# The first head's query remainder: from a VectorE subtraction to a TensorE matmul and a ScalarE copy

## What is computed

```python
x = x + tanh(g_xattn[0]) * xattn(layernorm(x), ctx, ctx, mask, Wq, Wk, Wv, Wo, 16)
x = x + tanh(g_ffn[0]) * ffn(layernorm(x), Wg, bg, W1, b1, W2, b2)
# xattn: 16 heads of 64, softmax(q k^T + mask) v, then Wo
# ffn: softmax over 8 experts, the best 2 of them, relu(x W1 + b1) W2 + b2, weighted
```

## Time and profile before

| | |
|---|---|
| median of 3 runs | 1154.83 us (1151.76 to 1156.01) |
| profiled execution | 1155.27 us, its span 1153.5 us |
| mean granted TensorE clock | 0.921 of full speed |
| busy: TensorE, VectorE, ScalarE, GpSimd | 881.5, 939.9, 785.6, 710.6 us |
| queries' low halves (L726) | 256, 681 ns each, 173.7 us |
| queries' high halves (L545) | 256, 599 ns each, 152.9 us |

### The profile page before, as it was taken

One profiled execution on the slowest core, in us unless ns is written; L12 is line 12 of the kernel. 1 busy time (PEld: TensorE's weight loads), 2 busy tenths in 40 slices (PEclk: granted clock), 3 DMA queues, 4 the chain that ended last, 5 costly groups with the idle time before them and its releaser, 6 DMA issues.

```text
span 1153.5 us, 33826 instructions
## 1 busy us (share of the span) xinstructions
PE 881.5 (76%) x11840; PEld 674.7 (58%) x11840; DVE 939.9 (81%) x2160; ACT 785.6 (68%) x1627; POOL 710.6 (62%) x701
## 2 busy tenths in 40 slices
PE   6787888798788888877897887878898767555560
PEld 4465665566566766666675656666676556444440
DVE  3888898898989897978888989978798987646633
ACT  3877778777677878786887667766887564444540
POOL 3143455547365666564658787755758787778775
PEclk9998899999999999999999998999998897778975
DMA  8367756555467765453445455554445465477773
GB/s 173 75 172 196 206 146 171 153 159 157 130 172 197 207 179 158 107 131 96 116 116 147 121 161 131 128 129 103 109 122 160 119 172 154 145 202 211 209 205 103
DMA packets 250791, 174.53 MB, mean 151 GB/s; under 512 B 39168, under 2 KB 232192, under 8 KB 250624
## 3 DMA queue, kind: packets, MB, share of 16 engines
q1 hardware_dynamic: 242432, 155.57, 50.9%
q0 software_dynamic: 8192, 16.79, 4.9%
HBM read 75.42 MB, written 63.84 MB: 121 GB/s over the span
## 4 chain that ended last, share of the span: by engine, by line
DVE 24%; issue 13%; PE 13%; POOL 8%; ACT 8%; SPq 3%; DMA 2%; DVEq 0%; POOLq 0%; ACTq 0%
PE bank L90 4%; POOL arena L1033 4%; PE bank L92 3%; PE bank L91 3%; DVE qL L726 3%; POOL hidL L1072 2%; DVE vL L901 2%; DVE row_max L929 2%; DVE otL L955 2%; DVE arena L909 2%; DVE x_back L949 2%; POOL slots L1020 2%; DVE row_sum L917 1%; SPq L1153 1%; ACT qH L545 1%
## 5 line engine op out<-in xcount | busy, mean ns | idle before, releaser
L1078 POOL TENSOR_TENSOR ptL<-pt,ptH 128x512 f16<-128x512 f32 x128 | 148.8, 1162 | 250.9 <-ACT pt L651 250.6
L726 DVE TENSOR_TENSOR qL<-bank,qH 128x512 f16<-128x512 f32 x256 | 173.7, 681 | 51.7 <-ACT qH L545 49.5
L545 ACT ACTIVATE qH<-bank 128x512 f16<-128x512 f32 x256 | 152.9, 599 | 43.8 <-PE bank L92 42.6
L1084 POOL TENSOR_TENSOR prob<-prob,row_inv 128x512 f32<-128x512 f32 x128 | 134.9, 1054 | 52.4 <-DVE row_inv L935 52.3
L1020 POOL DMA_INDIRECT slots<-x2hat,slot x128 | 128.1, 1001 | 31.9 <-issue 29.9
L90 PE MATMUL bank<-ptH,vdH 128*128 128x64 f16 x1024 | 120.4, 202 | 33.6 <-DVE arena L909 23.6
L1033 POOL DMA_INDIRECT arena<-slots,slot x128 | 123.1, 962 | 36.1 <-issue 29.7
L90 PE MATMUL bank<-arena,hidH 128*128 128x128 f16 x396 | 83.6, 240 | 69.6 <-POOL hidL L1072 66.9
L90 PEld LDWEIGHTS bank<-ptH,vdH 128*128 128x128 f16 x1024 | 107.9, 118 | 41.2 <-DVE arena L909 27.6
L1072 POOL TENSOR_TENSOR hidL<-arena,hidH 128x512 f16<-128x512 f32 x99 | 115.7, 1169 | 12.2 <-ACT hidH L595 10.8
L91 PE MATMUL bank<-ptL,vdH 128*128 128x64 f16 x1024 | 120.4, 202 | 0.0
(11 more groups left out here) (158 smaller groups left out, 3399.5 us busy)
## 6 DMA issues: line engine op xcount, KB each, us to landing
arena<-expert_weights SPq DMA_DIRECT2D x99, 321.0 KB, 3.1
slots<-zeros SPq DMA_DIRECT2D x60, 512.0 KB, 3.4
vdH<-vH SPq DMA_DIRECT2D x256, 64.0 KB
vdL<-vL SPq DMA_DIRECT2D x256, 64.0 KB
arena<-slots SPq DMA_DIRECT2D x99, 128.0 KB
slots<-arena SPq DMA_DIRECT2D x99, 128.0 KB
x_raw<-in_x SPq DMA_DIRECT2D x16, 256.0 KB, 4.1
ctx_raw<-in_ctx SPq DMA_DIRECT2D x16, 256.0 KB, 4.6
```

The source lines that it names most:

```text
L545: act.activation(qH[:, g % 2, 2 * j + g2, :, h2, :], bk("Q", g, h)[:, :].rearrange("p (b q) -> p b q", b=GB), ACT.Copy).then_inc(s_q_high, 1)
L726: dve.tensor_tensor(qL[at], bk("Q", g, h)[:, :].rearrange("p (b q) -> p b q", b=GB), qH[at], ALU.subtract).then_inc(s_q_low[h % 2], 1)
L1078: pool.tensor_tensor(ptL[:, b % 2, :], pt[:, b % 2, :], ptH[:, b % 2, :], ALU.subtract).then_inc(s_pt_low, 1)
L1084: pool.tensor_tensor(p, p, row_inv[:, b % NPB, :].unsqueeze(2).to_broadcast([P, JG, S]), ALU.mult).then_inc(s_normal, 1)
```

## The change

The low half of the first head of a step (`2i`) is no longer subtracted by VectorE. TensorE, between the scores and the probabilities' transposes, multiplies the high half by minus the identity and adds it onto the queries' bank; ScalarE, right after the high half of head `2i+1`, copies what is then in the bank as the low half. VectorE keeps the low half of head `2i+1`. GpSimd builds the table minus identity at the start. The counters of low halves are split accordingly: even heads by ScalarE, odd heads by VectorE.

```diff
+        minus_ident = sb("minus_ident", [P, P], F16)
...
+        s_q_rest, s_minus = sem("q_rest"), sem("minus_ident")
...
+            def queries_rest(g, h):
+                pe.wait_ge(s_q_high, g * H + h + 1)
+                if g == 0 and h == 0:
+                    pe.wait_ge(s_minus, 2)
+                j, h2, g2 = h // 4, h % 4 // 2, h % 2
+                pe.matmul(bk("Q", g, h)[:, :].rearrange("p (b q) -> p b q", b=GB), minus_ident[:, :],
+                          qH[:, g % 2, 2 * j + g2, :, h2, :], start=False, stop=True,
+                          skip_group_check=True).then_inc(s_q_rest, 1)
...
                 if within(s, B):
                     scores(s)
+                if within(g + 1, GROUPS):
+                    queries_rest(g + 1, 2 * i)
                 if within(s - 2, B):
                     transpose_probs(s - 2)
...
+            def queries_rest_low(g, h):
+                act.wait_ge(s_q_rest, g * H // 2 + h // 2 + 1)
+                j, h2, g2 = h // 4, h % 4 // 2, h % 2
+                act.activation(qL[:, g % 2, 2 * j + g2, :, h2, :], bk("Q", g, h)[:, :].rearrange("p (b q) -> p b q", b=GB),
+                               ACT.Copy).then_inc(s_q_low[0], 1)
...
                 if within(g + 1, GROUPS):
                     queries_high(g + 1, 2 * i + 1)
+                    queries_rest_low(g + 1, 2 * i)
                 if unit_at(s) is not None:
                     slots_high(unit_at(s))
...
-                                  ALU.subtract).then_inc(s_q_low[h % 2], 1)
+                                  ALU.subtract).then_inc(s_q_low[1], 1)
...
-                if within(g + 1, GROUPS):
-                    queries_low(g + 1, 2 * i)
                 if within(s // 2, TILES):
...
+            pool.memset(minus_ident[:, :], 0.0).then_inc(s_minus, 1)
+            pool.wait_ge(s_minus, 1)
+            pool.affine_select(out=minus_ident[:, :], in_=minus_ident[:, :], compare_op=ALU.not_equal, fill=-1.0, base=0,
+                               pattern=[[-1, P]], channel_multiplier=1).then_inc(s_minus, 1)
```

## The result

The changed kernel takes 1163.0 us (median of 20 runs, 1158.97 to 1170.88) against 1155.32 us (20 runs) for the kernel before on the same chip: ratio 1.0071, interval 1.0055 to 1.0087. The chip of a later comparison gave 1.0066 (1.0043 to 1.0088). The forecast, 1145 with a range of 1133 to 1161, is wrong in its sign.

What follows compares the result with a forecast made beforehand. No engine was full; the pace passed mostly through VectorE's queue, ScalarE leading at certain steps. Terms -6.2 - 3.1 - 1.2 + 0.3 = -10.2 us from 1155.27 gave 1145; own range 1137 to 1149, 8-in-10 range 1133 to 1161.

Steps and rivals of the forecast that it cites:

- VectorE's relief: VectorE's queue loses 128 subtractions of 0.60 us, 77 us as upper bound; gains 2.4 us per unit-free group, 0.88 with units.
- the walk at i=2 to 5: Group without units: VectorE is behind, each step gives 0.60, 2.4 us; catching up at i=3 and i=4 returns about 0.6.
- my own sign: Group without units, expected at 48.6 us: if not shorter by 1 us, the walk is wrong at i=2 to 5.
- the slots' step: At i=0 with slots to turn, priced from step 64: ScalarE's copy delays the slots' high half; cost 0.7 us.
- I take nothing: Queries' bank, now freed by ScalarE, before products with the values: bounds -0.60 and +0.48 us a step, counted as nothing.
- mostly waiting where the new matmul stands; I count nothing: TensorE's 128 new matmuls, 28 us, fall where it mostly waits; nothing counted but 0.2 us at i=7.
- where I had 0.3 us: Eight steps before the first scores: TensorE waits for ScalarE's high half, 0.4 us a step; bounds 0 and 3.3, taken 0.3.
- ScalarE's 0.48 us: Queue time of each of ScalarE's 128 new copies, 61 us in all; VectorE's queue covers about half at i=6.
- the slower one: Rival: ScalarE's copy waits behind the scores, ahead of the slots, and frees the queries' bank late; +7, 1162; chance 0.18.
- The Trainium skill's rule: Relieve the engine with the highest occupancy first, VectorE at 81%; by that alone all 77 us come off, leaving 1078.

Runs made afterwards that it cites:

- relief alone: Kernel before, with VectorE's subtraction for even heads left out and nothing in its place, bank free after ScalarE's high half: 1134.10 us, ratio 0.9828.
- the version with i=2, 3, 5: Changed kernel with the new path only at i=2, 3 and 5, not in the first group; VectorE's subtraction elsewhere: 1163.33 us, ratio 0.9930; again 0.9926.
- that with i=0, 4, 7: Changed kernel with the new path only at i=0, 4 and 7, from the second group on; VectorE's subtraction elsewhere: 1188.04 us, ratio 1.0152.
- that with i=6: Changed kernel with the new path only at i=6, from the second group on; VectorE's subtraction elsewhere: 1175.28 us, ratio 1.0048.
- relief and copy: Kernel before, with the even heads' subtraction left out and one more ScalarE copy per step from a table into a scratch tile: 1171.22 us, ratio 0.9987.
- i=2 and 3 alone: Kernel before, with the new path for the first head at i=2 and i=3 only, from the second group on: 1146.82 us, ratio 0.9929.

## Why the prediction was wrong

| built up | ratio | step |
|---|---|---|
| relief alone | 0.9828 | -19.9 us |
| and ScalarE's copy | 0.9987 | +1.6% |
| and the bank held until the copy | 1.0082 | +0.95% |
| and TensorE's wait | 1.0089 | within error |
| the change itself, with the matmul | 1.0071, 1.0066 | within error |

The steps of this ladder start from a bank that is free as soon as ScalarE's high half is made. In the kernel before it was free later. So the first row holds VectorE's relief and an earlier release, and the third takes this back and adds the delay of the change. How the two rows would divide against the release of the kernel before was not measured; that all of them together give the change's time was.

**Right in sum, and partly by luck: VectorE's relief.** My terms for it (2.4 us in each of 4 groups, 0.88 in each of 9, 1.2 in the combine) sum to 18.7 us; measured alone, 19.9. But by stages, in the profile of that kernel, steps 16 to 48 gave 3.6 us where I had 9.6, steps 48 to 112 10.0, and the steps up to 16 gave 5.0 where I had nothing; and the 19.9 us include the earlier release. The gain at i=2, 3, 5 is real: 0.7% in two versions.

**Right: the walk at i=2 to 5.** By my own sign, a group without units that is not shorter by 1 us would mean that the walk is wrong at i=2 to 5. The group got 0.7 us longer, and yet these steps hold. Between the starts of ScalarE's first high halves, i=2 to 5 took 28.73 us before and 27.09 in the changed kernel, -1.6 where I had -1.8 (-2.4 + 0.6). The steps i=6, 7, 0 and 1 went from 22.09 to 24.45 us, +2.4 where I had +0.23. The second profile of the change gives -2.3 and +2.7. The same kernel profiled on two chips differs by 0.5 and 0.9 us in these two sums, so what is clear is the miss of the second sum. The failure is in the four steps where ScalarE leads.

**Right: the slots' step.** ScalarE's stream in step 64 of the changed kernel, where the earlier trace rows has the one before:

```profile
458.32 0.60 ACT L558 ACTIVATE qH<-bank 128x512 f16<-128x512 f32 x1
...
462.06 0.60 ACT L564 ACTIVATE qL<-bank 128x512 f16<-128x512 f32 x1 [0.98 <-PE bank L355]
462.56 0.38 ACT L598 ACTIVATE slot_xtH<-bank 128x256 f16<-128x256 f32 x1
```

The step began at 458.32, before at 455.35:

```profile
455.35 0.60 ACT L545 ACTIVATE qH<-bank 128x512 f16<-128x512 f32 x1
```

The slots' high half stands 4.24 us after the start, before 2.83 (458.18): 1.4 us later, as forecast (459.6 against 458.18). VectorE's low half of the outputs in the same step:

```profile
464.63 0.68 DVE L973 TENSOR_TENSOR otL<-bank,otH 128x512 f16<-128x512 f32 x1
```

It stands 6.31 us after the start, before 5.64 (460.99): 0.67, where I had 0.7.

**Failed: "I take nothing" for the queries' bank.** In the table above this is the step that turns the sign. I gave it bounds of -0.60 and +0.48 us a step, one pitch of either engine, named only the products with the values as its next taker, and took the middle. Tied to ScalarE's copy instead of the high half, the release costs 11 us (0.95%). The bounds were of the wrong kind: the release moves by instructions of ScalarE's step, not by one pitch. From the end of the first high half to the end of the last read of its bank it took, in us, the mean of 16 groups:

| i | 0 | 1 | 2 | 3 | 4 | 5 | 6 | 7 |
|---|---|---|---|---|---|---|---|---|
| before (VectorE, L726) | 0.98 | 0.86 | 2.87 | 2.81 | 1.63 | 2.81 | 0.76 | 1.13 |
| changed (ScalarE, L564) | 3.06 | 2.45 | 2.71 | 2.65 | 2.73 | 2.51 | 2.40 | 2.87 |

Where VectorE is behind (i=2, 3, 5) the bank comes free 0.2 to 0.3 us sooner, as I had said. At i=6, 7, 0 and 1, where ScalarE leads, it comes free 1.6 to 2.1 us later, over three times my upper bound, and at i=4 1.1 us later. The experiments fall in line with that: the version with i=2, 3, 5 gains, that with i=0, 4, 7 and that with i=6 lose. At i=6 the next taker is the context's transposes, ahead of the next group's queries, and not only the products with the values. TensorE began them 1.40 us after ScalarE's high half had begun in the kernel before, 0.63 us after it with the bank free at once, and 3.19 us after it with the bank held.

**Failed: "mostly waiting where the new matmul stands; I count nothing".** TensorE was idle at that place on average, but the wait of the new instruction is for a half that ScalarE delivers late just at i=6 and i=1 (41.5 and 13.7 of the 58.0 us of idle time ahead of the matmul), and there TensorE had been running ahead. Alone, on the kernel before, it costs 0.65%; in the change it adds nothing that can be told beside the held bank (1.0082 without it, 1.0089 with it). It is seen in the start phase, where I had 0.3 us: 15.7 us without the wait and 17.6 with it (relief and copy, one chip). The arithmetic of the matmul (28 us of TensorE by my estimate) shows nowhere in the time: the change with it is no slower than the last kernel without it. The matmul was not run by itself.

**Mis-sized: ScalarE's 0.48 us.** My terms against the gain (0.6 + 0.23 in 4 groups, 0.8 or 0.33 in 9) sum to 8.2 us. Alone the copies cost 14.4; beside the relief the step in the table is about 18, and the two agree within their intervals. I had let VectorE's lag cover about half of it at i=6, 7 and 0 and hide it at i=4 and 5. Which of these was wrong no run shows by itself: the version with i=0, 4, 7 has the wait and the later release in it too.

The rivals: the slower one, 1162 at a chance of 0.18, met the time (1163) and named half of its mechanism, the bank that ScalarE frees late. Its other half, the slots' step, is real but small. That the number fits is luck: it still had the groups without units gain 6.2 us, where they lost 2.9, and put all of the loss, 13.5 us, into the groups with units. The Trainium skill's rule (Perfetto Trace Analysis, Identifying the Most-Contended Engine) pointed at VectorE, and relieving it at no cost, with the bank freed sooner, does give time, 1.7% and not 6.7%; relieving it by loading the engine that leads in the other steps gives nothing that can be told (0.9987).

## What to carry to other kernels

When work moves between engines in a hand-ordered pipeline, price three things apart: the queue time it leaves, the queue time it joins, and for each buffer it reads, how many instructions of the new engine now stand between the data and its release. Look for an engine that runs ahead at the place where a wait is put in: its average idle time is no cover if what it waits for is late in just those steps. And an exchange that loses over the whole loop can win in the steps where the giving engine leads: here i=2 and 3 alone give 0.7%.

## What the runs showed of the hardware

The time between the starts of two back-to-back 128x512 evictions was 0.60 us on VectorE and 0.48 us on ScalarE, against durations of 0.68 and 0.60 us; queue time is priced here with the former. ScalarE's copy of 128x512 f32 to f16 took 643 ns from SBUF (a broadcast of 256 columns) and 610 ns from PSUM. After 4.1 us in which TensorE waited, its next 4.3 us were granted a clock of 0.50; in the kernel before, after a wait of 2.04 us at the same place, the next 2.5 us were granted 0.72 and the 2.0 us after them 0.50.
